# Adding the residual unscaled: a per-source deviation in the edge weights and in the second norm's epsilon

## The chip, the cores and the metric

The kernel runs on one core of a Trainium2 chip. The metric is the device time of one execution in microseconds (us). The kernel before takes 849.54 us, the median of three runs (848.42 to 850.84).

## What is computed

128 graphs of 128 nodes with 128 features go through two blocks. Each block has a residual and a layer norm without gain or bias:

```
x1 = layernorm(x + gnn0(x))      # two graph convolutions, then four LSTM passes over node windows
out = layernorm(x1 + gat(x1))    # multi-head attention over 256 edges
# gat: Xq = x1 Wlin', Xv = x1 Wval'                      (per node, 4 heads of 32)
#      e  = a . leaky_relu(Xq[src] + Xq[dst]) + log(adj[src, dst] + 1e-8)
#      w  = softmax of e over the edges of one source
#      Y[src] = sum over edges of w * Xv[dst];  gat = Y Wout'
# layernorm(z) = (z - mean(z)) / sqrt(var(z) + 1e-5)
```

The change concerns the second block only. Let y be the centred row x + gnn0(x) of one node, s = sqrt(var + eps) its deviation and r = 1/s. Then x1 = r y, and x1 + gat is the same row as y + s gat up to the factor r. A layer norm doesn't see that factor if its epsilon is multiplied by s squared.

## The kernel before

The core's five engines run hand-written instruction streams joined by semaphores. The first part (`front`) computes gnn0 and takes most of the time. The second part (`back`) is a software pipeline over 32 tiles of 4 graphs (`BT`), in 48 slots numbered n. Each engine has a function `slot(n)` that issues its share of several tiles at different depths, and the order within it is written out by hand.

In slot n of `back`:

- TensorE makes queries and values of tile n (L1330, L1352), edge scores of tile n-1 (L1373), the sum over end nodes of tile n (L1363, L1364), the sum by source of tile n-14 (`sum_by_source`, L1407), its output product (`output`, L1418), and turns tile n+1 or n+2 (L1326). Every eighth slot (13, 21, 29, 37) `attention_by_edge` turns the softmax row (L1387) and spreads r of the edges' end nodes over the edges (L1390).
- ScalarE (ACT in the profile) orders and copies tiles (L1522, L1526, L1533), scales queries (L1511, L1515), copies the sum by source (L1552), and normalises output tiles (L1547). For the late tiles 19 to 30 it also multiplies the kept row by r (`scale_x`, L1558).
- VectorE (DVE) takes the statistics of entering tiles (`stats_in`, L1620), scales queries, does the softmax steps (L1652 to L1676), weights gathered values (L1700), adds the residual (`add_mixed` of tile n-15: L1710 with r as a scalar in four instructions for tiles 0 to 18, L1707 in one instruction for the late tiles), and takes the statistics of leaving tiles (`stats_out`, L1718). `attention_out` (L1682, L1686) multiplies the attention by r of the end node.
- GpSimd (POOL) turns statistics into factors. `factors(n)` serves tile n+2 on its way in and tile n-15 on its way out in one set of small instructions: L1253, L1255, L1256, L1258, L1260, L1261, L1263, L1265, a power of -1/2 (L1267) and the shift (L1274). It also normalises half of each output tile up to tile 18 (L1240), and issues the additions and gathers by DMA.
- The DMA queue of SyncE stores values and output tiles.

A tile's query needs its factors from POOL, and TensorE's sum by source of a tile needs the residual add of the tile before (`o_read`). `stats_out` in slot n waits for `factors` of slot n-2. Entering tiles end with slot 31; slots 32 to 47 drain the rest. The last tile leaves by `leave_last` in two halves.

Of the kernel before, what the change touches and what calls it, by code (L numbers as in the profile page):

```python
# [103 lines left out]
def front(nc, sb, sem, tables, hT_hi, hT_lo, ident, adj_sb, psum, xb, adj, Wg0, bg0, Wg1, bg1, Wih, Whh, bih, bhh,  # L104
# [101 lines left out]
             "adjT_psum adjT_ready degree_psum degree_ready by_ready ranks_psum deg_hi bias_hi ranks_cut "  # L206
             "b_summed b_psum b_ready wg1_cut wg1_ready w_psum w_hi_ready w_lo_ready "
# [111 lines left out]
    def run_tensor(pe, entry):  # L319
# [96 lines left out]
        def slot(n):  # L416
# [33 lines left out]
            if has(n - 3):  # L450
                k = n - 3
                if not k:
                    pe.wait_ge(S["wg1_ready"], 1)
# [219 lines left out]
    def run_vector(dve, entry):  # L673
# [16 lines left out]
        def rank_rows():  # L690
            dve.wait_ge(S["ranks_psum"], 1)
            bank = psum[:, GATE_BANK[I], :]
            dve.tensor_copy(deg_rows[:, :, :], bank[0:RANKS, 0:P].unsqueeze(2).broadcast_to([RANKS, P, BT])).then_inc(S["deg_hi"], 1)
            dve.tensor_copy(bias_rows[:, :], bank[0:RANKS, P:2 * P]).then_inc(S["bias_hi"], 1)
            dve.wait_ge(S["deg_hi"], 1)
# [3 lines left out]
            dve.wait_ge(S["bias_hi"], 1)  # L699
            lo = slice(BIAS_LO, BIAS_LO + 2)  # L700
            dve.tensor_tensor(bias_rows[lo], bank[lo, P:2 * P], bias_rows[lo].bitcast(F32), ALU.subtract).then_inc(S["ranks_cut"], 1)
            dve.tensor_copy(wg1_hi[:, :], wg1[:, :]).then_inc(S["wg1_cut"], 1)
            dve.wait_ge(S["wg1_cut"], 1)
            dve.tensor_tensor(wg1_lo[:, :], wg1[:, :], wg1_hi[:, :].bitcast(F32), ALU.subtract).then_inc(S["wg1_ready"], 1)
# [311 lines left out]
def back(nc, sb, sem, tables, before, hT_hi, hT_lo, ident, psum, xt, a, src, v_rows, values, out):  # L1016
# [18 lines left out]
    RING = LAG + 13  # L1035
# [3 lines left out]
    LOG_AT, EXP_AT = 4, 6  # L1039
# [9 lines left out]
    x1_kept = sb("x1_kept", [P, RING, BT, P])  # L1049
    yT = sb("yT", [P, 2, TW])  # L1050
# [6 lines left out]
    diff, mean_sum, m2_sum, half_diff, minus_mean, m2_eps, diff_sq, var_eps = (  # L1057
        sb(n, [P, 2, BT]) for n in ("diff", "mean_sum", "m2_sum", "half_diff", "minus_mean", "m2_eps", "diff_sq", "var_eps"))

    rstd = sb("rstd", [P, tiles + LAG + 4, 2, BT])  # L1060
    shift = sb("shift", [P, 2, BT])
    edge_rstd = sb("edge_rstd", [P, EC, GT, BT])
# [10 lines left out]
             "edge_rstd_ready attn_ready va_ready yt_psum yT_ready scaled_x o_psum o_read stats2_done "  # L1073
# [73 lines left out]
    def scale_of(k, b):  # L1147
        return rstd[:, k, 0, b:b + 1]

    def out_factors(m, b):  # L1150
        return rstd[:, m + 4 + LAG, 1, b:b + 1], shift[:, m % 2, b:b + 1]
# [71 lines left out]
    def run_gpsimd(pool):  # L1223
# [19 lines left out]
        def factors(n):  # L1243
# [6 lines left out]
            if leaving:  # L1250
                pool.wait_ge(S["stats2_done"], n - 2 - LAG + 1)
            st = stats[:, n % 2, w]
# [12 lines left out]
            pool.tensor_tensor(var_eps[:, w], m2_eps[:, w], diff_sq[:, w], ALU.add).then_inc(S["var_done"], 1)  # L1265
            pool.wait_ge(S["var_done"], done)
            op = pool.tensor_tensor(rstd[:, n + 2, w], var_eps[:, w], minus_half[:, w], ALU.pow)  # L1267
            if leaving:
                op.then_inc(S["rstd_done"], 1)
                m = n - 2 - LAG  # L1270
# [3 lines left out]
                op = pool.tensor_tensor(shift[:, m % 2], minus_mean[:, 1], rstd[:, n + 2, 1], ALU.mult)  # L1274
            op.then_inc(S["factors_done"], 1)

# [43 lines left out]
    def tensor_steps(pe):  # L1320
# [61 lines left out]
        def attention_by_edge(g):  # L1382
            pe.wait_ge(S["attn_row"], g + 1)
            if g:
                pe.wait_ge(S["va_ready"], EC * g * GT)
            for c in range(EC):
                mm = pe.transpose(attn[:, c, :], row_a[:, c * P:(c + 1) * P], ident[:, :])  # L1387
            for c in range(EC):
                at = EC * P + c * GT * BT
                mm = pe.matmul(psum[:, ATTN, at:at + GT * BT], to_r[:, c * P:(c + 1) * P].bitcast(F32),  # L1390
                               rstd[:, g * GT:(g + 1) * GT, 0, :], start=True, stop=True)
            mm.then_inc(S["attn_psum"], 1)

# [45 lines left out]
        def slot(n):  # L1439
# [8 lines left out]
            if has(n):  # L1448
                values(n)
                if behind_values(n):  # L1450
                    last_query(n)
            if new_group and has(n):
# [52 lines left out]
    def scalar_steps(act):  # L1505
# [66 lines left out]
        def slot(n):  # L1572
# [18 lines left out]
            elif has(n - 1 - LAG):  # L1591
                copy_yT(n - 1 - LAG)
                if late(n - 1 - LAG):
                    scale_x(n - 1 - LAG)
# [19 lines left out]
    def vector_steps(dve):  # L1614
# [8 lines left out]
        def query_hi(k):  # L1623
            dve.wait_ge(S["factors_done"], k + 1)
            dve.wait_ge(S["q_psum"], 2 * k + 2)
            if k:
                dve.wait_ge(S["linear_kept"], k)
            dve.tensor_tensor(xq_hi[:, 0:IN_BANK, :], psum[:, Q, 0:IN_BANK * QC].rearrange("p (b d) -> p b d", d=QC),
                              rstd[:, k, 0, 0:IN_BANK].unsqueeze(2).broadcast_to([P, IN_BANK, QC]), ALU.mult)
# [47 lines left out]

        def attention_out(g):
# [3 lines left out]
            dve.tensor_copy(edge_rstd[:, :, :, :], bank[:, EC * P:EC * (P + GT * BT)].rearrange("p (c k b) -> p c k b", c=EC, b=BT)).then_inc(  # L1682
                S["edge_rstd_ready"], 1)
            dve.wait_ge(S["edge_rstd_ready"], g + 1)
            for c in range(EC):
                op = dve.tensor_tensor(attn[:, c, :].rearrange("p (b k h) -> p b k h", b=BT, h=HEADS),  # L1686
                                       bank[:, c * P:(c + 1) * P].rearrange("p (b k h) -> p b k h", b=BT, h=HEADS),
                                       edge_rstd[:, c].rearrange("p k b -> p b k").unsqueeze(3).broadcast_to([P, BT, GT, HEADS]), ALU.mult)
# [32 lines left out]
        def leave_last():  # L1721

            for h, of_half in enumerate(halves):
                dve.wait_ge(S["last_o"], h + 1)
                for b in of_half:
                    op = dve.scalar_tensor_tensor(out=x1_kept[:, place(last), b, :], in0=x1_kept[:, place(last), b, :],
                                                  scalar=scale_of(last, b), in1=psum[:, last_out_bank[h], b * P:(b + 1) * P],
                                                  op0=ALU.mult, op1=ALU.add)
                op.then_inc(S["last_added"], 1)
# [10 lines left out]
            dve.tensor_scalar(last_var[:, :], last_moments[:, :, 1], LN_EPS, None, ALU.add).then_inc(S["last_normed"], 1)  # L1740
# [19 lines left out]
        def slot(n):  # L1760
# [35 lines left out]
            for step in STEPS[part][1] if part is not None else ():  # L1796
                softmax(g, step)
            if n == 1:
# [101 lines left out]
```

## Time and profile before

| | |
|---|---|
| median of three runs | 849.54 us |
| the profiled execution, whole | 849.15 us |
| its span in the trace | 847.2 us |
| busy: PE, DVE, ACT, POOL | 818.1, 672.7, 616.4, 257.8 us |
| `back` takes over from `front` | about 601 us |
| slots 15 to 29 | about 670 to 772 us |
| last instruction of POOL ends | about 842.8 us |

A busy time is that of an engine's recorded instructions. In the rows, L numbers are lines of the kernel, "x4" joins four records, and the part in square brackets is idle time of the engine just before the instruction, with what ended it.

### The profile page before, as it was taken

The page shows a single profiled execution, that of the slowest core. Times are in us where ns is not written, and L with a number is a line of the kernel's source. Part 1 is how long each engine was busy: PE and PEld are TensorE (multiplying, and loading weights), DVE is VectorE, ACT ScalarE, POOL GpSimd, SP SyncE. Part 2 cuts the span into 40 slices and gives each one's busy share as a digit, 9 for nine tenths or more (in the row PEclk, how much of TensorE's full clock was granted, in tenths as well). Part 3 has the DMA queues.
Part 4 walks back from the last instruction along what each step waited for, and adds up shares of the span by engine and source line. Part 5 has one row for each costly group of instructions (what it writes and reads, how often), then busy time and mean ns, then how long its engine had stood idle before and what let it go on. Part 6 is the DMA issues. An engine that isn't in the chain of part 4 may idle for free.

```text
span 847.2 us, 14387 instructions
## 1 busy us (share of the span) xinstructions
PE 818.1 (97%) x4882; PEld 701.8 (83%) x4882; DVE 672.7 (79%) x1494; ACT 616.4 (73%) x1109; POOL 257.8 (30%) x604
## 2 busy tenths in 40 slices
PE   8999999999999999999999999999999999999883
PEld 7888888877888878988887888878887899999783
DVE  5888888868888788777787776768777799898884
ACT  3788778886677776777676566666697688887686
POOL 0233333350000000000000010100577577777886
PEclk9999999999999999999999999999999999999997
DMA  5122221000000000100000047777418866534543
GB/s 144 62 67 61 62 63 50 14 1 1 2 0 1 1 1 5 46 1 1 1 1 0 1 100 183 164 180 167 126 63 231 243 188 187 200 125 163 162 169 93
DMA packets 37895, 70.54 MB, mean 83 GB/s; under 512 B 3360, under 2 KB 24512, under 8 KB 32704
## 3 DMA queue, kind: packets, MB, share of 16 engines
q0 software_dynamic: 4608, 33.56, 15.3%
q1 hardware_dynamic: 32288, 35.73, 13.5%
q8 instruction: 40, 0.66, 0.3%
q10 hardware_dynamic: 928, 0.35, 0.2%
q14 instruction: 31, 0.25, 0.1%
HBM read 36.06 MB, written 16.78 MB: 62 GB/s over the span
## 4 chain that ended last, share of the span: by engine, by line
PE 82%; ACT 6%; POOL 6%; DVE 3%; issue 2%; DMA 1%; POOLq 0%; DVEq 0%; ACTq 0%
PE psum L514 9%; PE psum L515 9%; PE psum L516 9%; PE psum L532 7%; PE psum L528 7%; PE psum L529 6%; PE psum L1407 3%; PE psum L424 3%; PE psum L466 3%; PE psum L401 2%; PE psum L400 2%; PE psum L399 2%; PE psum L1330 2%; PE psum L1352 2%; PE psum L1363 2%
## 5 line engine op out<-in xcount | busy, mean ns | idle before, releaser
L654 ACT ACTIVATE work<-psum,bias 128x512 f32<-128x512 f32 (+2 forms) x364 | 229.0, 666 | 35.8 <-PE psum L532 31.8
L514 PE MATMUL psum<-hT_hi,w_hi 128*128 128x512 f32 (+2 forms) x362 | 139.6, 386 | 1.2 <-ACT work L654 1.2
L515 PE MATMUL psum<-hT_lo,w_hi 128*128 128x512 f32 (+2 forms) x362 | 139.3, 385 | 0.0
L516 PE MATMUL psum<-hT_hi,w_lo 128*128 128x512 f32 (+2 forms) x362 | 139.1, 384 | 0.0
L635 ACT ACTIVATE work<-work 128x512 f32<-128x512 f32 (+1 forms) x100 | 61.3, 613 | 94.9 <-DVE work L977 58.6
L1228 POOL DMA_DIRECT2D hT_lo<-hT_hi x8 | 7.6, 947 | 339.5 <-DVE hT_lo L924 320.2
L988 DVE TENSOR_TENSOR work<-work 128x512 f32<-128x512 f32 (+1 forms) x99 | 66.7, 673 | 47.7 <-ACT work L635 47.7
L528 PE MATMUL psum<-hs_hi,w_hi 128*128 128x512 f32 (+2 forms) x256 | 98.3, 384 | 0.3 <-DVE hs_hi L922 0.3
L532 PE MATMUL psum<-hs_lo,w_hi 128*128 128x512 f32 (+2 forms) x256 | 98.5, 385 | 0.0
L529 PE MATMUL psum<-hs_hi,w_lo 128*128 128x512 f32 (+2 forms) x256 | 97.8, 382 | 0.0
L970 DVE TENSOR_TENSOR work<-work 128x512 f32<-128x512 f32 (+1 forms) x100 | 66.4, 664 | 20.6 <-ACT work L654 20.5
L514 PEld LDWEIGHTS psum<-hT_hi,w_hi 128*128 128x128 f32 x362 | 68.3, 189 | 16.0 <-ACT work L654 1.5
L593 ACT ACTIVATE work<-psum,bias 128x512 f32<-128x512 f32 x96 | 65.7, 688 | 21.7 <-PE psum L401 19.0
L516 PEld LDWEIGHTS psum<-hT_hi,w_lo 128*128 128x128 f32 x362 | 68.2, 189 | 13.5
L515 PEld LDWEIGHTS psum<-hT_lo,w_hi 128*128 128x128 f32 x362 | 68.2, 188 | 13.0
L1407 PE MATMUL psum<-from_node,values 128*128 128x128 f32 x496 | 60.8, 276 | 5.1 <-DVE x_kept L1710 3.4
L1407 PEld LDWEIGHTS psum<-from_node,values 128*128 128x128 f32 x496 | 57.8, 192 | 5.8 <-issue 3.7
L1267 POOL TENSOR_TENSOR rstd<-var_eps,minus_half 128x4 f32<-128x4 f32 (+1 forms) x48 | 60.5, 1260 | 3.8
L314 POOL CAST hT_hi<-work 128x512 fp32r<-128x512 f32 x32 | 20.0, 624 | 125.3 <-DVE work L850 125.3
L532 PEld LDWEIGHTS psum<-hs_lo,w_hi 128*128 128x128 f32 x256 | 48.1, 188 | 11.2 <-DVE hs_lo L924 2.1
L528 PEld LDWEIGHTS psum<-hs_hi,w_hi 128*128 128x128 f32 x256 | 48.2, 188 | 10.3 <-DVE hs_hi L922 1.5
L529 PEld LDWEIGHTS psum<-hs_hi,w_lo 128*128 128x128 f32 x256 | 48.2, 188 | 9.2
(238 smaller groups left out, 1898.5 us busy)
## 6 DMA issues: line engine op xcount, KB each, us to landing
work<-x_by_batch SPq DMA_DIRECT2D x32, 256.0 KB, 2.6
x_stage<-x_by_state SPq DMA_DIRECT2D x8, 1024.0 KB, 5.7
hT_lo<-hT_hi POOLq DMA_DIRECT2D x8, 1024.0 KB, 8.7
hT_lo<-x_stage POOLq DMA_DIRECT2D x8, 1024.0 KB, 7.2
v_rows<-values SPq DMA_DIRECT2D x32, 256.0 KB, 2.4
out<-x_kept SPq DMA_DIRECT2D x31, 256.0 KB, 2.4
work<-L_gnn_Wih SPq DMA_DIRECT2D x4, 256.0 KB, 2.9
work<-L_gnn_Whh SPq DMA_DIRECT2D x3, 256.0 KB, 3.1
```

Source lines behind the costliest of these rows:

```text
L514: pe.matmul(out, w_hi[:, w, g, :], xh, start=True, stop=False)
L515: pe.matmul(out, w_hi[:, w, g, :], xl, start=False, stop=False)
L516: mm = pe.matmul(out, w_lo[:, w, g, :], xh, start=False, stop=(t == 0))
L528: pe.matmul(out, w_hi[:, w, g, :], hh, start=False, stop=False)
L529: pe.matmul(out, w_lo[:, w, g, :], hh, start=False, stop=False)
L532: pe.matmul(out, w_hi[:, w, g, :], hl, start=False, stop=True).then_inc(gate_psum[g], 1)
L593: op = act.activation(gate[1][g], psum[:, GATE_BANK[g], :], ACT.Tanh if g == G else ACT.Sigmoid, bias=bias[:, g:g + 1])
L635: act.activation(tanh_c[k % 2][:, 0:ph.width(tile)], cell[k % 2][:, 0:ph.width(tile)], ACT.Tanh).then_inc(S["tanh_ready"], 1)
L654: op = act.activation(gate[s][g][:, 0:ph.width(tile)], psum[:, 4 * s + g, 0:ph.width(tile)], ACT.Tanh if g == G else ACT.Sigmoid, bias=bia ...
L970: op = dve.tensor_tensor(i_g, gate[s][I][:, 0:ph.width(tile)], gate[s][G][:, 0:ph.width(tile)], ALU.mult)
L988: dve.tensor_tensor(h_full[s][:, 0:ph.width(tile)], gate[s][O][:, 0:ph.width(tile)], tanh_c[s][:, 0:ph.width(tile)], ALU.mult).then_inc(S[ ...
L1407: mm = pe.matmul(psum[:, sum_bank(k), b * P:(b + 1) * P], va_of(k, c, b), from_node[:, c, :], start=(c == 0), stop=(c == EC - 1))
```

## The change

The residual is added unscaled: `add_mixed` and `leave_last` add the attention's output to the kept row in one instruction per tile or half, and `scale_x` is gone. The edge weights are multiplied by s of the source as well as by r of the end node. For that, two transposes in slot 9 and one VectorE copy make the one-hot table of sources (`from_r`); GpSimd forms s and eps s^2 for eight tiles at a time (`late_scales`, slots 8, 16, 24, 32); TensorE spreads s over the edges by two more products a group; VectorE multiplies once more. GpSimd's `factors` adds the kept eps s^2 in an instruction of its own. The rings of factors and of kept rows are re-sized (26 to 25 kept rows), and a few semaphores of `front` are merged, with the same instructions between them.

```diff
 def factors(n):   # GpSimd, "leaving": a tile on its way out is served
             if leaving:
                 pool.tensor_scalar(minus_mean[:, 1], mean_sum[:, 1], -0.5, None, ALU.mult)
-            pool.tensor_scalar(m2_eps[:, w], m2_sum[:, w], 1.0 / P, LN_EPS, ALU.mult, ALU.add).then_inc(S["scaled"], 1)
+                pool.tensor_scalar(m2_mean[:, w], m2_sum[:, w], 1.0 / P, None, ALU.mult).then_inc(S["scaled"], 1)
+                pool.wait_ge(S["std_ready"], m // GT + 1)
+            else:
+                pool.tensor_scalar(m2_eps[:, w], m2_sum[:, w], 1.0 / P, LN_EPS, ALU.mult, ALU.add).then_inc(S["scaled"], 1)
             pool.wait_ge(S["scaled"], done)
+            if leaving:
+                pool.tensor_tensor(m2_eps[:, w], m2_mean[:, w], late_eps[:, m % KEPT, w], ALU.add)
             pool.tensor_tensor(diff_sq[:, w], half_diff[:, w], half_diff[:, w], ALU.mult).then_inc(S["squared"], 1)
...
+        def late_scales(g):
+            pool.wait_ge(S["factors_done"], GT * (g + 1))
+            if g:
+                pool.wait_ge(S["attn_psum"], g)
+            pool.tensor_tensor(std[:, :, :], var_kept[:, kept, 0], rstd[:, of_group, 0], ALU.mult)
+            pool.tensor_scalar(late_eps[:, kept, 1], var_kept[:, kept, 0], LN_EPS, None, ALU.mult).then_inc(S["std_ready"], 1)
...
 GpSimd, slot n, after factors(n)
+            if n and n % GT == 0 and n // GT <= groups:
+                if n == GT:
+                    pool.memset(late_eps[:, :, 0], LN_EPS)
+                late_scales(n // GT - 1)
...
         def attention_by_edge(g):
             pe.wait_ge(S["attn_row"], g + 1)
+            pe.wait_ge(S["std_ready"], g + 1)
...
+            for c in range(EC):
+                at = EC * P + (EC + c) * GT * BT
+                mm = pe.matmul(psum[:, ATTN, at:at + GT * BT], from_r[:, c * P:(c + 1) * P], std[:, :, :], start=True, stop=True)
             mm.then_inc(S["attn_psum"], 1)
+        def turn_sources():            # slot 9
+            for c in range(EC):
+                mm = pe.transpose(attn[:, c, :], from_node[:, c, :], ident[:, :])
+            mm.then_inc(S["from_psum"], 1)
...
-        def scale_x(m):
-            act.wait_ge(S["stats_done"], m + 1)
-            for b in range(BT):
-                kept = x1_kept[:, place(m), b, :]
-                op = act.activation(kept, kept, ACT.Copy, scale=scale_of(m, b))
-            op.then_inc(S["scaled_x"], 1)
...
+        def keep_sources():            # slot 9
+            dve.wait_ge(S["from_psum"], 1)
+            dve.tensor_copy(from_r[:, :], psum[:, ATTN, 0:E]).then_inc(S["from_ready"], 1)
...
 def attention_out(g):
+            dve.tensor_copy(edge_scale[:, :, :, :], of_ends[0]).then_inc(S["edge_scale_ready"], 1)
+            dve.wait_ge(S["edge_scale_ready"], 2 * g + 1)
+            dve.tensor_tensor(edge_scale[:, :, :, :], edge_scale[:, :, :, :], of_ends[1], ALU.mult).then_inc(S["edge_scale_ready"], 1)
...
         def add_mixed(m):
             dve.wait_ge(S["o_psum"], m + 1)
-            if late(m):
-                dve.wait_ge(S["scaled_x"], m - first_late + 1)
-                kept = x1_kept[:, place(m)]
-                dve.tensor_tensor(kept, kept, by_bank(out_bank(m)), ALU.add).then_inc(S["o_read"], 1)
-                return
-            for b in range(BT):
-                op = dve.scalar_tensor_tensor(out=x1_kept[:, place(m), b, :], in0=x1_kept[:, place(m), b, :], scalar=scale_of(m, b),
-                                              in1=psum[:, out_bank(m), b * P:(b + 1) * P], op0=ALU.mult, op1=ALU.add)
-            op.then_inc(S["o_read"], 1)
+            kept = x1_kept[:, place(m)]
+            dve.tensor_tensor(kept, kept, by_bank(out_bank(m)), ALU.add).then_inc(S["o_read"], 1)
```

## Rows read from the trace of the kernel before

**Rows 1.** The page: the chain that ended last, its shares by engine

```profile
PE 82%; ACT 6%; POOL 6%; DVE 3%; issue 2%; DMA 1%; POOLq 0%; DVEq 0%; ACTq 0%
```

**Rows 2.** Windows: stretch, length, busy us of PE, PEld, DVE, ACT, POOL; clock, DMA

```profile
666.00:774.00 108.00, 107.98 (x972) 99.48 (x973) 95.41 (x339) 88.70 (x186) 76.84 (x190) 1.00 0.56 182
...
812.00:843.00 31.00, 20.75 (x172) 19.44 (x171) 20.76 (x65) 27.11 (x76) 26.48 (x93) 0.91 0.31 98
```

**Rows 3.** Timeline of POOL: start us, length us, instruction; one round of `factors`

```profile
819.62 0.20 POOL L1253 TENSOR_TENSOR diff<-stats 128x4 f32<-128x4 f32 x1
819.77 0.20 POOL L1255 TENSOR_TENSOR mean_sum<-stats 128x4 f32<-128x4 f32 x1
...
820.22 0.23 POOL L1258 TENSOR_SCALAR half_diff<-diff 128x4 f32<-128x4 f32 x1
820.41 0.22 POOL L1260 TENSOR_SCALAR minus_mean<-mean_sum 128x4 f32<-128x4 f32 x1
820.69 0.19 POOL L1261 TENSOR_SCALAR m_eps<-m_sum 128x4 f32<-128x4 f32 x1
820.97 0.20 POOL L1263 TENSOR_TENSOR diff_sq<-half_diff 128x4 f32<-128x4 f32 x1
...
822.78 0.20 POOL L1253 TENSOR_TENSOR diff<-stats 128x4 f32<-128x4 f32 x1
```

**Rows 4.** Timeline around 772 us: what POOL's last idle time waited for

```profile
772.88 0.60 ACT L1533 ACTIVATE x_kept<-psum 128x512 f32<-128x512 f32 x1
...
773.51 0.87 DVE L1620 BATCH_NORM_STATS2 stats<-x_kept 128x6 f32<-128x128 f32 x4
...
774.46 0.21 POOL L1253 TENSOR_TENSOR diff<-stats 128x8 f32<-128x8 f32 x1 [2.42 <-DVE stats L1620]
```

**Rows 5.** Groups by line, all of `back`: count, busy us, mean ns

```profile
L1710 DVE SCALAR_TENSOR_TENSOR x_kept<-x_kept,rstd,psum 128x128 f32<-128x128 f32 x76 | 21.2, 341 | 8.4 <-PE psum L1418 8.3
...
L1240 POOL TENSOR_SCALAR x_kept<-x_kept,rstd,shift 128x128 f32<-128x128 f32 x38 | 18.7, 496 | 1.9 <-POOL shift L1274 0.2
...
L1558 ACT ACTIVATE x_kept<-x_kept,rstd 128x128 f32<-128x128 f32 x48 | 15.3, 398 | 0.0
...
L1707 DVE TENSOR_TENSOR x_kept<-x_kept,psum 128x512 f32<-128x512 f32 x12 | 8.1, 674 | 0.0
```

**Rows 6.** Timeline of PE, slot 29: attention by edge and what follows

```profile
767.16 0.38 PE L1387 MATMUL psum<-ident,row_a 128*128 128x128 f32 x2
767.38 0.53 PE L1390 MATMUL psum<-rstd,to_r 128*128 128x32 f32 x4
...
767.74 2.03 PE L1407 MATMUL psum<-from_node,values 128*128 128x128 f32 x16
```

**Rows 7.** Timeline of DVE, slots 9 and 13

```profile
646.04 0.57 DVE L1628 TENSOR_TENSOR xq_hi<-psum,rstd 128x396 fp32r<-128x396 f32 x1 [0.28 <-issue]
...
663.12 0.22 DVE L1682 COPY edge_rstd<-psum 128x64 f32<-128x64 f32 x1
663.38 0.50 DVE L1686 TENSOR_TENSOR psum<-psum,edge_rstd 128x128 f32<-128x128 f32 x2
```

**Rows 8.** Timeline of PE, slots 13 and 14

```profile
662.46 0.39 PE L1363 MATMUL psum<-ends,xq_hi 128*128 128x256 f32 x1 [0.50 <-DVE xq_lo L1643]
...
666.02 2.05 PE L1407 MATMUL psum<-from_node,values 128*128 128x128 f32 x16 [0.49 <-DVE values L1700]
```

**Rows 9.** Timeline of DVE and POOL around 791 us

```profile
791.23 0.69 DVE L1657 TENSOR_TENSOR_SCAN row_a<-cap_f,rows 128x256 f32<-128x256 f32 x1
...
791.36 0.57 POOL L1260 TENSOR_SCALAR minus_mean<-mean_sum 128x4 f32<-128x4 f32 x1
```

**Rows 10.** Timeline in the drain: PE, DVE, ACT

```profile
787.71 2.02 PE L1407 MATMUL psum<-from_node,values 128*128 128x128 f32 x16 [2.52 <-DVE x_kept L1710]
...
820.56 1.27 DVE L1700 TENSOR_TENSOR values<-values,psum 128x512 f32<-128x512 f32 x2
...
835.54 1.65 ACT L1547 ACTIVATE x_kept<-x_kept,shift,rstd 128x128 f32<-128x128 f32 x4 [0.85 <-POOL shift L1274]
```

More of the change, by code:

```diff
@@ L1034, in back @@
     LAG = GT + 5
-    RING = LAG + 13
+    RING = LAG + 12
+    FACTORS, KEPT = 3 * GT, 2 * GT
     GROUP = before.phases[-1].sizes[0] // BT
@@ L1049, in back @@
     x1_kept = sb("x1_kept", [P, RING, BT, P])
+    from_r = sb("from_r", [P, E])
+    late_eps = sb("late_eps", [P, KEPT, 2, BT])
+    std = sb("std", [P, GT, BT])
+    spare = sb("spare", [P, 96])
     yT = sb("yT", [P, 2, TW])
@@ L1056, in back @@
     stats = sb("stats", [P, 2, 2, BT, 6])
-    diff, mean_sum, m2_sum, half_diff, minus_mean, m2_eps, diff_sq, var_eps = (
-        sb(n, [P, 2, BT]) for n in ("diff", "mean_sum", "m2_sum", "half_diff", "minus_mean", "m2_eps", "diff_sq", "var_eps"))
-    rstd = sb("rstd", [P, tiles + LAG + 4, 2, BT])
+    diff, mean_sum, m2_sum, half_diff, minus_mean, m2_mean, m2_eps, diff_sq = (
+        sb(n, [P, 2, BT]) for n in ("diff", "mean_sum", "m2_sum", "half_diff", "minus_mean", "m2_mean", "m2_eps", "diff_sq"))
+    rstd = sb("rstd", [P, FACTORS, 2, BT])
+    var_kept = sb("var_kept", [P, KEPT, 2, BT])
     shift = sb("shift", [P, 2, BT])
-    edge_rstd = sb("edge_rstd", [P, EC, GT, BT])
+    edge_scale = sb("edge_scale", [P, EC, GT, BT])
     last_stats, last_moments = sb("last_stats", [P, BT, 6]), sb("last_moments", [P, BT, 2])
@@ L1072, in back @@
              "z_psum leaky_ready edges_psum log_taken log_added max_f max_b below_max exp_done sum_f sum_b recip_done attn_row attn_psum "
-             "edge_rstd_ready attn_ready va_ready yt_psum yT_ready scaled_x o_psum o_read stats2_done "
+             "edge_scale_ready attn_ready va_ready yt_psum yT_ready from_psum from_ready std_ready o_psum o_read stats2_done "
              "halves scaled squared var_done rstd_done factors_done out_act out_pool "
@@ L1147, in scale_of @@
     def scale_of(k, b):
-        return rstd[:, k, 0, b:b + 1]
+        return rstd[:, k % FACTORS, 0, b:b + 1]
     def out_factors(m, b):
-        return rstd[:, m + 4 + LAG, 1, b:b + 1], shift[:, m % 2, b:b + 1]
+        return rstd[:, (m + 4 + LAG) % FACTORS, 1, b:b + 1], shift[:, m % 2, b:b + 1]
     def region_free(engine):
@@ L1251, in factors @@
                 pool.wait_ge(S["stats2_done"], n - 2 - LAG + 1)
+            m = n - 2 - LAG
+            at, kept = (n + 2) % FACTORS, (n + 2) % KEPT
             st = stats[:, n % 2, w]
@@ L1260, in factors @@
                 pool.tensor_scalar(minus_mean[:, 1], mean_sum[:, 1], -0.5, None, ALU.mult)
-            pool.tensor_scalar(m2_eps[:, w], m2_sum[:, w], 1.0 / P, LN_EPS, ALU.mult, ALU.add).then_inc(S["scaled"], 1)
+                pool.tensor_scalar(m2_mean[:, w], m2_sum[:, w], 1.0 / P, None, ALU.mult).then_inc(S["scaled"], 1)
+                pool.wait_ge(S["std_ready"], m // GT + 1)
+            else:
+                pool.tensor_scalar(m2_eps[:, w], m2_sum[:, w], 1.0 / P, LN_EPS, ALU.mult, ALU.add).then_inc(S["scaled"], 1)
             pool.wait_ge(S["scaled"], done)
+            if leaving:
+                pool.tensor_tensor(m2_eps[:, w], m2_mean[:, w], late_eps[:, m % KEPT, w], ALU.add)
             pool.tensor_tensor(diff_sq[:, w], half_diff[:, w], half_diff[:, w], ALU.mult).then_inc(S["squared"], 1)
             pool.wait_ge(S["squared"], done)
-            pool.tensor_tensor(var_eps[:, w], m2_eps[:, w], diff_sq[:, w], ALU.add).then_inc(S["var_done"], 1)
+            pool.tensor_tensor(var_kept[:, kept, w], m2_eps[:, w], diff_sq[:, w], ALU.add).then_inc(S["var_done"], 1)
             pool.wait_ge(S["var_done"], done)
-            op = pool.tensor_tensor(rstd[:, n + 2, w], var_eps[:, w], minus_half[:, w], ALU.pow)
+            op = pool.tensor_tensor(rstd[:, at, w], var_kept[:, kept, w], minus_half[:, w], ALU.pow)
             if leaving:
                 op.then_inc(S["rstd_done"], 1)
-                m = n - 2 - LAG
                 pool.wait_ge(S["rstd_done"], m + 1)
@@ L1273, in factors @@
                     pool.wait_ge(S["out_act"], m - 1)
-                op = pool.tensor_tensor(shift[:, m % 2], minus_mean[:, 1], rstd[:, n + 2, 1], ALU.mult)
+                op = pool.tensor_tensor(shift[:, m % 2], minus_mean[:, 1], rstd[:, at, 1], ALU.mult)
             op.then_inc(S["factors_done"], 1)
+        def late_scales(g):
+            of_group, kept = slice(g * GT % FACTORS, g * GT % FACTORS + GT), slice(g * GT % KEPT, g * GT % KEPT + GT)
+            pool.wait_ge(S["factors_done"], GT * (g + 1))
[3 more added lines that the diff above has]
+            pool.tensor_scalar(late_eps[:, kept, 1], var_kept[:, kept, 0], LN_EPS, None, ALU.mult).then_inc(S["std_ready"], 1)
         def gather_values(j):
@@ L1451, in slot @@
                     last_query(n)
+            if n == SOURCES_AT:
+                turn_sources()
             if new_group and has(n):
@@ L1681, in attention_out @@
             dve.wait_ge(S["attn_psum"], g + 1)
-            dve.tensor_copy(edge_rstd[:, :, :, :], bank[:, EC * P:EC * (P + GT * BT)].rearrange("p (c k b) -> p c k b", c=EC, b=BT)).then_inc(
-                S["edge_rstd_ready"], 1)
-            dve.wait_ge(S["edge_rstd_ready"], g + 1)
+            of_ends = [bank[:, EC * P + j * EC * GT * BT:EC * P + (j + 1) * EC * GT * BT].rearrange("p (c k b) -> p c k b", c=EC, b=BT)
+                       for j in range(2)]
+            dve.tensor_copy(edge_scale[:, :, :, :], of_ends[0]).then_inc(S["edge_scale_ready"], 1)
+            dve.wait_ge(S["edge_scale_ready"], 2 * g + 1)
+            dve.tensor_tensor(edge_scale[:, :, :, :], edge_scale[:, :, :, :], of_ends[1], ALU.mult).then_inc(S["edge_scale_ready"], 1)
+            dve.wait_ge(S["edge_scale_ready"], 2 * g + 2)
             for c in range(EC):
@@ L1724, in leave_last @@
                 dve.wait_ge(S["last_o"], h + 1)
[L1725 to L1729, printed above, removed]
+                at = slice(of_half.start, of_half.stop)
+                kept = x1_kept[:, place(last), at, :]
+                dve.tensor_tensor(kept, kept, by_bank(last_out_bank[h])[:, at, :], ALU.add).then_inc(S["last_added"], 1)
             for h, of_half in enumerate(halves):
@@ L1739, in leave_last @@
             dve.wait_ge(S["last_normed"], 2)
-            dve.tensor_scalar(last_var[:, :], last_moments[:, :, 1], LN_EPS, None, ALU.add).then_inc(S["last_normed"], 1)
+            dve.wait_ge(S["std_ready"], groups)
+            dve.tensor_tensor(last_var[:, :], last_moments[:, :, 1], late_eps[:, last % KEPT, 1], ALU.add).then_inc(S["last_normed"], 1)
             dve.wait_ge(S["last_scaled"], 1)
@@ L1797, in slot @@
                 softmax(g, step)
+            if n == SOURCES_AT:
+                keep_sources()
             if n == 1:
```

32 lines of the change are left out of this document (16 added, 16 removed).

## The prediction

> **What bounds the kernel now.** I began with the page's shares and its chain of waits. PE has 82% of the chain, ACT and POOL 6% each, DVE 3% [rows 1]. The two engines that the change relieves, ACT and DVE, are the question; so I cut `back` into stretches (the view by windows) and read the timeline of each engine in them. The median is 849.54 us; the profiled execution took 849.15, so sums made on it are carried over to the median by adding the difference that they give. The kernel can be told from an unchanged one from about 0.3%, 2.55 us, on.
>
> Stretch A, slots 15 to 29, 666 to 774 us: PE is busy 107.98 of 108.00 us at full clock, DVE 95.41, POOL 76.84 [rows 2]. Whatever leaves DVE there is worth nothing unless PE waits for it, and what is added to PE counts in full.
>
> Stretch B, from 774.46 us to the end of POOL's work at about 842.8 us: POOL waits for the last time at 774.46 us, for the statistics of slot 30 [rows 4]. From there its timeline has no idle time but the short issue gaps around two pairs of gathers. It makes 17 rounds of `factors` (n = 29 to 45), up to n = 34 with the normalising of half a tile between them. In the drain a round takes 822.78 - 819.62 = 3.16 us [rows 3], again and again. ACT's round is as long by chance: a copy step of 0.5, four scalings (4 x 0.398 = 1.6 as lengths, about 1.17 in steps), four normalisings of 1.65. But at 835.54 it is ACT that waits, 0.85 us, for POOL's shift [rows 10], and POOL, which waits for nobody, is the last to finish. So the view of the chain, which names ACT for part of the drain, has two equally long loops to choose from, and only POOL's reaches back to 774 us unbroken.
>
> **The change part by part.**
>
> *Removed from ACT:* 48 scalings, 12 tiles of 4 [rows 5]. All lie in stretch B, next to a POOL that is never free. Worth 0; if POOL were not there, see the second rival.
>
> *Removed from DVE:* 76 scaled additions (19 tiles of four, 0.341 us each; in the timeline a tile steps on by about 1.12 us) become 19 whole ones as L1707, 0.674 us [rows 5]. That is 0.45 us a tile, 8.5 us of DVE time. In stretch A PE is full, so 0. At the seam, slot 30: the statistics of tile 31 start at 773.51, after the addition, but also only after ACT's copy of the tile, which ends at 772.88 + 0.60 = 773.48 [rows 4]. An earlier addition leaves the start where it is: 0. In stretch B PE does wait for an addition, 2.52 us before 787.71 [rows 10], but PE is not what ends the stretch: 0 again. The last tile's two halves gain some tenths beside POOL's last rounds: 0.
>
> *Added to PE:* each group gets two more products of the form L1390 (two matmuls, four records). The old ones take from 767.38 to 767.74, 0.36 us [rows 6]; the two transposes of slot 9 are priced by L1387, 767.38 - 767.16 = 0.22 us [rows 6]. Place by place:
> - slot 9: 0.22. PE runs without a gap there. The copy that DVE adds in that slot (about 0.4 us) falls on 0.28 us of idle time [rows 7] plus the 0.22 us by which PE is itself later, so it is covered.
> - slot 13: PE waits 0.50 us for xq_lo behind the attention [rows 8], which hides the 0.36. But DVE's additional multiplication sits between the copy and the weighting: one step of 663.38 - 663.12 = 0.26 us [rows 7], and at 666.02 PE waits 0.49 us for exactly those weighted values [rows 8]. So 0.26.
> - slots 21 and 29: 0.36 each, PE being full. DVE's step of 0.26 there is less than the 0.45 it saves in the same slot.
> - slot 37: in stretch B, beside POOL: 0.
> Sum on PE: 0.22 + 0.26 + 0.36 + 0.36 = 1.20 us. Bounds: 0.7 (only slots 21 and 29 count) to 1.5.
>
> *Added to POOL, in each leaving round:* before, minus_mean to m_eps takes 0.28 us and m_eps to diff_sq 0.28 [rows 3], the second across a wait. After, m2_mean takes the place of m_eps but has one operation, as minus_mean has after half_diff, where the step is 0.19 [rows 3]. Its length should be like minus_mean's, 0.03 more than m_eps, so the step across the wait becomes 0.31. Then m2_eps, a two-input instruction with no wait before diff_sq: a step as from diff to mean_sum, 0.15 to 0.16 [rows 3]. New: 0.19 + 0.31 + 0.155 = 0.65 against 0.56, so +0.09 a round. The added wait for `std_ready` was satisfied slots ago (late_scales of that group ran at least 7 slots before), and everything queued behind it waits for m2_mean anyhow. Bounds for a round: 0.06 (m2_mean as short as m_eps) and 0.25 (two operations or one make no difference, and the additional wait costs 0.1). I take 0.09, since each of its steps has a like step in the same round. 17 rounds: 1.5 us, from 1.0 to 4.3. In stretch A the rounds have slack (POOL 71% busy [rows 2]): 0.
>
> *Added to POOL, late_scales:* groups 0 to 2 fall into slots 8, 16 and 24, where POOL has waits to spare: 0. The fourth falls into slot 32, inside stretch B, after the round and before a normalising: two instructions of 128x32. They lie between 0.20 us (128x4 [rows 3]) and 0.50 (128x128, L1240 [rows 5]) each; nearer the first, 0.22, so about 0.45 us for the pair, bounds 0.3 to 1.0. Its wait for attn_psum is long met (slot 29). Behind it in POOL's queue stand normalise_out and the next round, so all of it counts.
>
> *What the phase does:* at 791.36 minus_mean took 0.57 instead of 0.22, ending just as DVE's scan of 791.23 + 0.69 does [rows 9]. Five POOL instructions between 791 and 801 us are stretched like this, 1.8 us together, each beside a DVE instruction of the fourth softmax with both inputs in SBUF. Those DVE instructions stay, but DVE will be about 0.5 to 1 us earlier against POOL's rounds. If all of them fell on POOL's long power, 1.8 us would be won; if none did, about 1 us more be lost. I book 0. The Trainium skill (SBUF — State Buffer, section "SBUF: two separate sides") says the same of the mechanism: VectorE with two SBUF inputs and GpSimd take one port pair in turn, and the loser waits for the whole instruction. By that rule the new additions, which read one operand from PSUM, block POOL no more than the old ones; no row here contradicts it, since the stretched ones stand beside scans and SBUF-only products alone.
>
> [...]
>
> Sum: 1.20 + 1.5 + 0.45 = 3.15 us. 849.15 + 3.15 = 852.3 for the profiled execution; on the median 849.54 + 3.1 = 852.6, or 0.36% slower.
>
> **The rivals.**
>
> *Most of it is hidden (no change that can be measured).* PE's additions count in slots 21 and 29 only (0.7), the rounds cost 1.0, late_scales 0.3, and DVE's earlier scans fall on POOL's power for 0.9 us: 0.7 + 1.0 + 0.3 - 0.9 = +1.1, 850.7. For it: PE has stalls in slots 13 and 14 [rows 8]. Against: POOL's additions lie on an engine that never idles.
>
> *ACT sets the drain (faster).* If the chain's reading is right and POOL merely keeps step with ACT, then 12 rounds of 3.16 us lose ACT's scaling, and the next loop is DVE's: two weightings 1.27 [rows 10], an addition 0.67, four statistics 0.87 as in [rows 4], 2.8 us. 12 x 0.37 = 4.4 us won, 1.2 lost on PE: -3.3, 846.3. It decides from the point on where POOL's round could be shorter than ACT's. Against it: POOL's steps are the same 3.16 with ACT waiting for it as without, and the 0.85 us of ACT [rows 10].
>
> *POOL pays more.* The upper bounds of the round: 17 x 0.25 = 4.3, with 1.2 and 0.6: +6.1, 855.7. For it: a wait more per round, and two where the order of satisfied and open waits is new. Against: the added wait has been satisfied for several slots when POOL reaches it, and it comes while m2_mean is still running.
>
> **How the numbers follow.** The forecast 0.55 (its own range 851.3 to 854.5; 0.45 of it beyond 2.55 us, 0.10 within); hidden 0.29; ACT's drain 0.07, of which 0.01 within; POOL pays more 0.09. Slower 0.45 + 0.09 = 0.54; same 0.10 + 0.29 + 0.01 = 0.40; faster 0.06. Eight in ten: 849.9 to 855.3, from below the hidden case to just short of the dearest one.
>
> **What would show it.** The slots of stretch A at the same PE step (about 6.7 us) with L1390's sibling 0.36 us longer in slots 21 and 29, POOL's last idle time about 1.2 us later than 774.46; POOL's round 3.25 in the drain with ACT now waiting for the shift in every round; no L1558, and DVE and PE idle more. I am wrong if POOL shows idle time in its rounds after slot 30 or its round is shorter than 3.16; if POOL's last idle time comes no later; or if the first instruction that waits for the added `std_ready` does so for a measurable time.

## The result and the profile after

The changed kernel takes 853.32 us, the median of 13 runs (851.99 to 853.80), against 849.54 us before (13 runs, 848.22 to 851.13). The ratio is 1.0043, with a 95% interval of 1.0035 to 1.0051: 3.7 us slower. Forecast were 852.6 us and slower.

Seen coarsely, the pages differ by what the change says: ACT is busy 603.8 us (616.4 before) and DVE 666.5 (672.7), PE 824.4 (818.1) and POOL 262.5 (257.8), in a span of 851.6 (847.2). The chain of waits of the changed kernel, shares by engine, no longer gives ACT its 6% [rows 1]:

```profile
PE 82%; POOL 8%; ACT 3%; DVE 3%; issue 2%; DMA 0%; POOLq 0%; DVEq 0%; ACTq 0%
```

One round of `factors` in the drain, timeline of POOL of the changed kernel (start, length, instruction), against [rows 3]:

```profile
829.56 0.20 POOL L1261 TENSOR_TENSOR diff<-stats 128x4 f32<-128x4 f32 x1
...
830.35 0.22 POOL L1268 TENSOR_SCALAR minus_mean<-mean_sum 128x4 f32<-128x4 f32 x1
830.53 0.22 POOL L1269 TENSOR_SCALAR m_mean<-m_sum 128x4 f32<-128x4 f32 x1
830.90 0.20 POOL L1275 TENSOR_TENSOR m_eps<-m_mean,late_eps 128x4 f32<-128x4 f32 x1
831.05 0.20 POOL L1276 TENSOR_TENSOR diff_sq<-half_diff 128x4 f32<-128x4 f32 x1
...
832.87 0.20 POOL L1261 TENSOR_TENSOR diff<-stats 128x4 f32<-128x4 f32 x1
```

The round takes 832.87 - 829.56 = 3.31 us where it took 3.16. m_mean starts 0.18 after minus_mean (0.28 for m_eps before), m_eps 0.37 after m_mean, diff_sq 0.15 after m_eps.

`late_scales` in slot 32 and POOL's last idle time, same view, with one line of the timeline of DVE at the end:

```profile
776.33 0.21 POOL L1261 TENSOR_TENSOR diff<-stats 128x8 f32<-128x8 f32 x1 [2.71 <-DVE stats L1649]
...
796.23 0.20 POOL L1286 TENSOR_TENSOR shift<-minus_mean,rstd 128x4 f32<-128x4 f32 x1
796.38 0.25 POOL L1295 TENSOR_TENSOR std<-var_kept,rstd 128x32 f32<-128x32 f32 x1
796.70 0.31 POOL L1296 TENSOR_SCALAR late_eps<-var_kept 128x32 f32<-128x32 f32 x1
796.98 1.24 POOL L1246 TENSOR_SCALAR x_kept<-x_kept,rstd,shift 128x128 f32<-128x128 f32 x2
797.21 0.76 DVE L1689 TENSOR_TENSOR_SCAN row_b<-cap_b,row_a 128x256 f32<-128x256 f32 x1
```

Normalising now starts 0.75 us after the shift. In the kernel before that step is 0.31 us in the same slot (793.95 to 794.26), so the pair costs 0.44. The last two lines show the stretching of [rows 9] too: the two rows of a half tile take 1.24 us there and 0.88 elsewhere, and a scan of DVE with two SBUF inputs stands beside them from 797.21 to 797.97.

PE in slot 21 of the changed kernel, against [rows 6] (the two differ only in slot):

```profile
714.18 0.53 PE L1418 MATMUL psum<-rstd,to_r 128*128 128x32 f32 x4
714.54 0.61 PE L1422 MATMUL psum<-std,from_r 128*128 128x32 f32 x4
714.99 2.03 PE L1443 MATMUL psum<-from_node,values 128*128 128x128 f32 x16
```

From the first record of one line to the first of the next, the old products take 0.36 and the new ones 0.45. That is a matter of the place and not of the table. The same view from 714.38 us and from 715.36 us on leaves out the first record of the old products and that of the sum by source:

```profile
714.21 0.50 PE L1418 MATMUL psum<-rstd,to_r 128*128 128x32 f32 x3
...
715.18 1.84 PE L1443 MATMUL psum<-from_node,values 128*128 128x128 f32 x15
```

The second old record starts 0.03 us after the first (714.18, 714.21), every later one of both tables 0.11 us after the one before it, and the second record of the sum 0.19 us after its first (714.99, 715.18). So each of the eight narrow records costs 0.11 us, 0.45 for four; of the old four, 0.08 us stands in the line behind them. In the kernel before it is the same (the first two records of [rows 6]'s L1390 start at 767.38 and 767.41, those of its L1407 at 767.74 and 767.94).

How this adds up can be read from the start of the values product of each slot (L1352 before, L1377 after); the difference between the two executions moves only at four places:

| slots | later than before, us | what lies at the step |
|---|---|---|
| 0 to 9 | 0.48 | the front part, see e8_front_only |
| 10 to 14 | 0.69 to 0.73 | transposes in slot 9: 0.21 |
| 15 to 21 | 0.97 | DVE's added product ahead of slot 14's wait: 0.25 |
| 22 to 29 | 1.42 | added products in slot 21: 0.45 |
| 30, 31 | 1.86 | added products in slot 29: 0.44 |

And ACT, relieved of its scalings, waits. The view of the waits from 776 us on (engine and line, waited for: us in total, times, longest), first of the kernel before:

```profile
ACT x_kept L1547 <- POOL shift L1274: 7.3, 5, 2.8
...
ACT x_kept L1585 <- POOL shift L1286: 16.6, 11, 4.4
```

One thing in this profile is not explained by the change's code. TensorE's granted clock was at the lower of its two levels (1.2 and not 2.4 GHz) from 790.5 to 793.9 us, which it was not in the profile of the kernel before. The view by windows, PE alone (stretch, length, busy us, granted clock, DMA), the kernel before first:

```profile
790.50:793.90 3.40, 2.91 (x26) 1.00 0.75 257
...
790.50:793.90 3.40, 3.40 (x21) 0.50 0.87 321
```

Ahead of it PE had waited 2.10 us for DVE's addition, up to 789.16; in the kernel before it waited 2.52 us at that place [rows 10] and the clock stayed up. The profiles of e4_no_pool_part (789.1 to 792.5) and e5_after_act_norm (787.6 to 791.0) have such a fall, those of the other kernels have none between 785 and 800 us, the changed kernel's relatives e2, e3, e7 and e10 among them. So no run shows that the change brings it. Here it makes DVE wait 3.55 us for PE's scores ahead of the softmax at 793.47, where it waited 2.30 before; POOL waits for none of them there and isn't held up, but DVE's scans come later against its rounds.

**Bookkeeping.** Two numbers of each profiled execution carry the reading: A, the start of POOL's round after its last long wait (774.46 before), and B, from there to the start of its last power (`last_rstd`, 841.79 before). A contains the front part, which differs between executions of any kernel; B doesn't. Of the time, the ratio with its interval is the safer reading: the executions of one kernel fall into groups (of the kernel before, near 848.2, 849.4 and 850.9 us), so that a median of a few can jump by 1 us.

| kernel | time, us | ratio to before (95%) | A | B | round |
|---|---|---|---|---|---|
| before | 849.54 | | 774.46 | 67.33 | 3.16 |
| changed | 853.32 | 1.0043 (1.0035 to 1.0051) | 776.33 | 69.78 | 3.31 |
| e1_no_scaling | 848.46 | 0.9993 (0.9984 to 1.0001) | 773.55 | 67.02 | 3.16 |
| e2_no_source_scale | 852.16 | 1.0031 (1.0020 to 1.0043) | 775.07 | 69.88 | 3.31 |
| e3_wait_ahead | 852.13 | 1.0033 (1.0021 to 1.0046) | 776.62 | 69.05 | 3.24 |
| e4_no_pool_part | 849.92 | 1.0012 (1.0004 to 1.0021) | 775.06 | 67.41 | 3.16 |
| e8_front_only | 849.38 | 1.0004 (0.9995 to 1.0013) | 774.52 | 67.33 | 3.17 |
| e5_after_act_norm | 851.31 | 1.0027 (1.0014 to 1.0039) | 774.75 | 69.04 | 3.31 |
| e6_before_act_norm | 848.47 | 0.9996 (0.9986 to 1.0006) | 774.68 | 66.39 | 3.16 |
| e7_both | 850.27 | 1.0013 (1.0003 to 1.0022) | 776.00 | 66.56 | 3.24 |
| e11_before_order_alone | 848.02 | 0.9986 (0.9977 to 0.9995) | 773.43 | 67.05 | 3.16 |
| e9_before_order | 847.21 | 0.9965 (0.9952 to 0.9979) | 774.71 | 65.21 | 3.17 |
| e10_after_order | 848.76 | 0.9985 (0.9976 to 0.9994) | 776.46 | 65.53 | 3.26 |
| e12_no_scaling_order | 846.51 | 0.9965 (0.9953 to 0.9977) | 775.11 | 64.29 | 3.17 |

Each was timed in five rounds against the kernel before, whose own medians were 849.05 to 849.54. B of the changed kernel is 2.45 us longer: 17 rounds x 0.15 = 2.55, late_scales 0.44, and 0.5 back by how DVE's two-input instructions fall on POOL's (between 790 and 803 us five of POOL's are stretched in either kernel, by 1.8 us together before and by 1.2 in the changed one). A less the start of slot 0 leaves the front part out: it is 169.2 to 169.3 us in all eight kernels without PE's part and 170.6 to 170.7 in all six with it.

### The profile page after: what moved, and what is told of

It is laid out like the page before. It is cut to its first block, busy times and chain, and to the rows that moved or that the text cites. A ratio compares the mean times of both kernels' runs of the same rounds, so it can differ in the third digit from the quotient of the medians.

```text
span 851.6 us, 14386 instructions
## 1 busy us (share of the span) xinstructions
PE 824.4 (97%) x4900; PEld 707.5 (83%) x4900; DVE 666.5 (78%) x1440; ACT 603.8 (71%) x1061; POOL 262.5 (31%) x644
## 4 chain that ended last, share of the span: by engine, by line
PE 82%; POOL 8%; ACT 3%; DVE 3%; issue 2%; DMA 0%; POOLq 0%; DVEq 0%; ACTq 0%
PE psum L514 9%; PE psum L515 9%; PE psum L516 9%; PE psum L532 7%; PE psum L528 7%; PE psum L529 6%; PE psum L424 4%; PE psum L1443 3%; PE psum L466 3%; PE psum L401 2%; PE psum L399 2%; PE psum L400 2%; PE psum L1355 2%; POOL rstd L1280 2%; PE psum L1377 2%
## 5 line engine op out<-in xcount | busy, mean ns | idle before, releaser
L515 PEld LDWEIGHTS psum<-hT_lo,w_hi 128*128 128x128 f32 x362 | 68.1, 188 | 13.1
L1443 PE MATMUL psum<-from_node,values 128*128 128x128 f32 x496 | 63.8, 284 | 4.4 <-DVE values L1736 2.2
L1443 PEld LDWEIGHTS psum<-from_node,values 128*128 128x128 f32 x496 | 60.7, 200 | 5.2 <-DVE values L1736 4.9
L1280 POOL TENSOR_TENSOR rstd<-var_kept,minus_half 128x4 f32<-128x4 f32 (+1 forms) x48 | 59.5, 1240 | 3.8
```

The lines of the kernel that those rows point to most:

```text
L515: pe.matmul(out, w_hi[:, w, g, :], xl, start=False, stop=False)
L1280: op = pool.tensor_tensor(rstd[:, at, w], var_kept[:, kept, w], minus_half[:, w], ALU.pow)
L1443: mm = pe.matmul(psum[:, sum_bank(k), b * P:(b + 1) * P], va_of(k, c, b), from_node[:, c, :], start=(c == 0), stop=(c == EC - 1))
```

## The experiments

**Is the relief of ACT and DVE worth anything?** The kernel before, without any scaling of the kept rows:

```diff
         def add_mixed(m):
-            if late(m):
-                dve.wait_ge(S["scaled_x"], m - first_late + 1)
...
+            kept = x1_kept[:, place(m)]
+            dve.tensor_tensor(kept, kept, by_bank(out_bank(m)), ALU.add).then_inc(S["o_read"], 1)
...
-                if late(n - 1 - LAG):
-                    scale_x(n - 1 - LAG)
```

> The kernel before, with the scaling of the kept rows left out (no scaling on ACT for tiles 19 to 30, a plain whole-tile addition on VectorE for tiles 0 to 30), so what is added to the attention's output is the unscaled row; nothing else changes. If POOL's unbroken run from slot 29 on sets the end, the relief of ACT and DVE is worth nothing: 849.5, within 0.7 us of before. If ACT sets the drain, as the chain of waits named it, it is 3 to 5 us faster: about 846.

Measured 848.46 us, ratio 0.9993, interval 0.9984 to 1.0001: at most 1.4 us, and no difference can be told. B is 67.02 against 67.33, the round the same 3.16 us. 13.1 us of busy ACT time (616.4 to 603.3) and 7.7 us of DVE time (672.7 to 665.0) left the kernel for no gain that can be told. The rival in which ACT sets the drain is out.

**What does PE's part cost?** The changed kernel without the deviation of the source in the edge weights:

```diff
-                mm = pe.matmul(psum[:, ATTN, at:at + GT * BT], from_r[:, c * P:(c + 1) * P], std[:, :, :], start=True, stop=True)
...
-                turn_sources()
...
-                keep_sources()
...
-            dve.tensor_tensor(edge_scale[:, :, :, :], edge_scale[:, :, :, :], of_ends[1], ALU.mult).then_inc(S["edge_scale_ready"], 1)
```

> The changed kernel, with the deviation of the source left out of the edge weights: no transposes and copy in slot 9, no two added products a group on PE, no added multiplication on DVE; GpSimd's additions stay. By the traces PE's place by place delays sum to 0.21 (slot 9) + 0.25 (slot 14) + 0.45 (slot 21) + 0.44 (slot 29) = 1.35 us, all ahead of stretch B: 1.35 us less than the changed kernel's 853.3, so 852.0. If PE's additions were hidden, 853.3.

Measured 852.16 us, 1.16 below the changed kernel (1.0 by the ratios, whose intervals overlap: the trace has to decide). The slots' starts are now later than before by the same amount from slot 0 (0.58) to slot 31 (0.61): all four steps of the table are gone. B is 69.88, like the changed kernel's, so PE's part acts on A alone.

**Does the satisfied wait cost something?**

```diff
 def factors(n):
             entering, leaving = has(n + 2), 0 <= n - 2 - LAG < last
+            if leaving and (n - 2 - LAG) % GT == 0:
+                pool.wait_ge(S["std_ready"], (n - 2 - LAG) // GT + 1)
...
-                pool.wait_ge(S["std_ready"], m // GT + 1)
```

> The changed kernel, with GpSimd's wait for std_ready made once a group ahead of the round and not in each round between m2_mean and m2_eps. The step across the wait is 0.37 us in the changed kernel where I expected 0.31. If the second wait costs the 0.06 to 0.07, the round falls from 3.31 to 3.24 us and 17 rounds save 1.1 us: 852.2. If an already satisfied wait costs nothing (the theory of the prediction) the time stays at 853.3 and the 0.37 is due to m2_mean.

Measured 852.13 us, 1.2 below the changed kernel; by the ratios it is 0.9, and their intervals overlap, so the time alone doesn't show a gain. The timeline of POOL in this kernel:

```profile
827.16 0.22 POOL L1271 TENSOR_SCALAR m_mean<-m_sum 128x4 f32<-128x4 f32 x1
827.46 0.20 POOL L1276 TENSOR_TENSOR m_eps<-m_mean,late_eps 128x4 f32<-128x4 f32 x1
```

The step from m_mean to m_eps falls from 0.37 to 0.30, and the round to 3.24. So this wait, whose count was reached slots ago, costs 0.07 us where it stands between an instruction and one that depends on it. 17 x 0.07 = 1.2 us would be gained by it; B falls by only 0.73, the scans again falling otherwise (the shift of slot 32 takes 0.51 us here, at 796.41, and 0.20 in the changed kernel).

**What does POOL's part cost?** The changed kernel with `factors` as before and constants for s and the second epsilon:

```diff
-                pool.tensor_scalar(m2_mean[:, w], m2_sum[:, w], 1.0 / P, None, ALU.mult).then_inc(S["scaled"], 1)
-                pool.wait_ge(S["std_ready"], m // GT + 1)
-            else:
-                pool.tensor_scalar(m2_eps[:, w], ...
+            pool.tensor_scalar(m2_eps[:, w], m2_sum[:, w], 1.0 / P, LN_EPS, ALU.mult, ALU.add).then_inc(S["scaled"], 1)
...
-                late_scales(n // GT - 1)
+                pool.memset(std[:, :, :], 1.0)
+                pool.memset(late_eps[:, :, :], LN_EPS).then_inc(S["std_ready"], 1)
```

> The changed kernel, with GpSimd's part left out: factors as before, no late_scales; s is a constant 1 and the second norm's epsilon unscaled. PE's and DVE's additions stay. If POOL's additions are 17 x 0.15 + 0.6 = 3.1 us and nothing hides them: 853.3 - 3.1 = 850.2, or up to 0.6 us more since the stretched instructions of slots 32 to 34 fall otherwise. If the cost is all on PE or in front: 853.

Measured 849.92 us, 3.4 below the changed kernel, B back at 67.41. Against the kernel before the ratio is 1.0012 (0.4 to 1.8 us), PE's part. The two parts together, 1.2 + 3.4 = 4.6, are somewhat more than the 3.7 to be explained; the uncertainty of each is near 1 us, and by the ratios they are 1.0 + 2.6 = 3.6. POOL is not quite unbroken here: at 796.16 it waits 0.39 us for DVE's statistics, after the lower clock of 789.1 to 792.5 us.

**Is the 0.48 us ahead of slot 0 the merged semaphores?** The kernel before, with the front part of the changed one:

```diff
-            dve.wait_ge(S["deg_hi"], 1)
+            dve.wait_ge(S["ranks_hi"], 1)
...
-                    pe.wait_ge(S["wg1_ready"], 1)
+                    pe.wait_ge(S["wg1_ready"], 2)
```

> The kernel before with only the merged semaphores of the front part from the changed one. In the profiled executions the back part begins 0.49 us later in the changed kernel. If that is the merged semaphores, 850.0; if it is how executions of any kernel differ from one another (others lie at -0.9 to +0.8 us there), 849.5 as before.

Measured 849.38 us, 1.0004 (0.9995 to 1.0013): no cost that can be told, at most 1.1 us. In its profile slot 0 starts 0.08 us later than before, and in those of all the others between 1.1 us earlier (e5_after_act_norm) and 0.8 us later (e3_wait_ahead).

**Where is time to be had?** If POOL sets stretch B, work that ACT can do should leave it. Two kernels, from the changed one and from the one before:

```diff
+    def by_act_alone(m):
+        return m >= 15
...
-            if has(n - 3 - LAG) and not late(n - 3 - LAG):
+            if has(n - 3 - LAG) and not by_act_alone(n - 3 - LAG):
                 normalize_out(n, n - 3 - LAG)
...
-            for b in range(BT if late(m) else HALF):
+            for b in range(BT if by_act_alone(m) else HALF):
```

> The changed kernel, with output tiles 15 to 18 normalised wholly by ACT and not half by GpSimd: four pairs of L1240 leave POOL's run in slots 31 to 34, each a step of about 1.0 us (0.85 and a wait). If POOL alone sets the end there, 853.3 - 4.0 = 849.3. VectorE has 3.55 us of idle time in one piece and little else between 784 and 812 us, and comes next: if it takes over, the gain is 2.5 to 3.5, so 850 to 851.

Measured 851.31 us: 2.0 less (1.4 by the ratios), short of both numbers. Of the 4 us that left POOL, 2.95 came back as waits: 1.08 for ACT's normalising (793.53) and 1.87 for DVE's statistics (796.18). The profile has the lower clock from 787.6 to 791.0 us, in which PE's sum by source takes 3.65 us and not 2.02, so a part of the second wait may belong to this execution alone (e7_both below, without the fall at that place, waits 1.08 us there).

> The kernel before with the same move (output tiles 15 to 18 normalised wholly by ACT). POOL theory alone: 849.5 - 4.0 = 845.5. Here VectorE is busy 33 of 38 us between 774 and 812 us with the scaled additions still on it and ACT's round is as long as POOL's: if these take over, the gain is 2 to 2.5: about 847.3. If ACT's round sets the end it isn't faster at all.

Measured 848.47 us, 0.9996: nothing that can be told, where 2 to 4 us were expected. The timeline of POOL of e6_before_act_norm shows where it went:

```profile
792.25 0.20 POOL L1277 TENSOR_TENSOR shift<-minus_mean,rstd 128x4 f32<-128x4 f32 x1 [0.44 <-ACT x_kept L1550]
...
795.33 0.51 POOL L1256 TENSOR_TENSOR diff<-stats 128x4 f32<-128x4 f32 x1 [2.88 <-DVE stats L1721]
```

Of the 4 us that left POOL, 3.3 came back as waits, 2.88 of it for DVE's statistics of slot 33. In slot 32 DVE weights two tiles ahead (four instructions, 2.5 us) before the addition for which PE waits (the 2.52 us of [rows 10]); whether that makes the statistics late is tried below.

With the wait ahead of the round as well, from the changed kernel:

> The changed kernel with both: the wait for std_ready once a group, ahead of the round, and output tiles 15 to 18 normalised wholly by ACT. If the two add up: 852.1 - (gain of the second alone, 2.5 to 4) = 848.1 to 849.6. The relief of ACT and DVE could be worth something only here, where POOL is shorter.

Measured 850.27 us, 3.05 below the changed kernel; the second measure gave 1.9 on top of e3. The added up range of 848.1 to 849.6 was missed for a like reason: POOL waits 1.08 us for DVE in slot 33.

**Is it DVE's order?** In slot 32 the weightings of tiles 19 and 20 go behind the addition and the statistics:

```diff
-            if not new_group:
+            if not new_group and n != tiles:
                 for k in ahead:
                     weight_values(k, 0)
                     weight_values(k, 1)
...
                 stats_out(n, n - 2 - LAG)
+            if n == tiles:
+                for k in ahead:
+                    weight_values(k, 0)
+                    weight_values(k, 1)
```

> The kernel before with output tiles 15 to 18 normalised by ACT alone, and in slot 32 VectorE weights tiles 19 and 20 after its residual addition and statistics and not ahead of them. Moving the normalising alone gave 0.6 us, since POOL then waited 2.9 us for VectorE's statistics behind the four weightings (2.5 us). If that wait is what ate the gain, this is 2 to 3 us faster than that kernel: 846. If POOL's run isn't what sets the end once shortened (ACT's equally long round), 848.5.

Measured 847.21 us, ratio 0.9965 (0.9952 to 0.9979): the fastest of the kernels that leave nothing out, 2.3 us below the kernel before (3.0 by the ratio), though not the 846 that I expected. The order accounts for a part of the wait: it fell from 2.88 to 1.81 us, and B by 1.18. The addition of slot 32 no longer stands behind the four weightings, but at 785.48 it waits 1.09 us for PE's output product.

> The changed kernel with the wait ahead of the round, tiles 15 to 18 normalised by ACT alone, and the same order on VectorE in slot 32. It had 850.3 us without the order, with POOL waiting 1.1 us for VectorE there: 1 us or a little more less, 849. Compared with the previous one, POOL's 17 x 0.08 + 0.6 and PE's 1.35 us remain as the change's cost, 3.3 us in all, unless ACT's free time is now worth something.

Measured 848.76 us, 0.9985. Faster than the kernel before, but 1.6 us behind its sister, and not 3.3. A says where: 776.46 against 774.71, PE's part of about 1.4 us and the front. B is 65.53 against 65.21: nearly equal, though a round is 0.09 longer. POOL's waits for DVE in the two, both from the timeline of POOL; first e9_before_order:

```profile
794.19 0.51 POOL L1256 TENSOR_TENSOR diff<-stats 128x4 f32<-128x4 f32 x1 [1.81 <-DVE stats L1721]
```

In e10_after_order the same instruction starts at 795.63 with no idle time before it, behind a stretched `late_scales`:

```profile
794.88 0.79 POOL L1300 TENSOR_SCALAR late_eps<-var_kept 128x32 f32<-128x32 f32 x1
795.63 0.45 POOL L1266 TENSOR_TENSOR diff<-stats 128x4 f32<-128x4 f32 x1
```

> The kernel before with VectorE's order in slot 32 alone. POOL is never idle there, so by the theory an earlier VectorE is worth nothing but for how its scans fall on POOL's instructions: 849.3, within 1 us either way. By the rival (PE's 2.52 us wait for the addition is on the path) 847.

Measured 848.02 us, 0.9986 (0.9977 to 0.9995). This lies between the two expectations and is a small gain that B doesn't explain: 67.05 against 67.33. The rest of the span's difference lies ahead of A in that execution, nearly all of it (0.99 us) ahead of slot 0. It remains open whether the order alone is worth more than some tenths.

**Does the relief pay once POOL is shorter?**

> The kernel before with output tiles 15 to 18 normalised by ACT alone and VectorE's order in slot 32, and with the scaling of the kept rows left out as in e1_no_scaling. With POOL unbroken the relief was worth nothing. In e9_before_order POOL waits 1.81 us once for VectorE's statistics, behind the scaled additions and the weightings; in the changed kernel's sister (e10_after_order) that wait is gone. If the relief pays where POOL is shortened, POOL's run from its last wait of slot 30 to its last power falls from 65.21 to about 63.5 us and the time to 845.7. If the wait has another cause, 847.2 stays.

In its timeline POOL's wait of slot 33 is 0.82 us:

```profile
793.68 0.51 POOL L1256 TENSOR_TENSOR diff<-stats 128x4 f32<-128x4 f32 x1 [0.82 <-DVE stats L1712]
```

The wait fell by 1.0 us and B by 0.92, to 64.29, half of what I expected. The median is 846.51 against 847.21 of e9, the ratios to before are the same 0.9965: in the profile the relief has become worth about 1 us, in the time it can't be told from none.

## Why the prediction was right, step by step

- *PE full in stretch A, its additions counted in full.* Right. The places were the four named; slot 9's 0.22 was 0.21, slot 14's 0.26 was 0.25. Slots 21 and 29 cost 0.45 and 0.44 and not 0.36, and the sum is 1.35 and not 1.20. The reading of [rows 6] was at fault and not the likeness: the step of 0.36 from L1390 to L1407 holds one record start of 0.03 us, and the 0.08 that it lacks stand in L1407's first step of 0.19.
- *POOL unbroken from slot 30's wait to the end; ACT and DVE relieved for nothing.* Right: e1_no_scaling shows it for the relief, and e4_no_pool_part shows the other side, as 2.6 to 3.4 us go with POOL's additions. One run is left over: e11_before_order_alone, 0.4 to 2.0 us faster though nothing was taken off POOL and B is only 0.28 shorter.
- *POOL's round +0.09.* The mis-sized term: it was +0.15, 17 x 0.06 = 1.0 us too little. The step with the one-operation m2_mean (0.18 to 0.19) and the step to diff_sq (0.15) were as read; the step across the wait was 0.37 and not 0.31. The sentence that failed is that the added wait costs nothing because it was satisfied slots ago. e3_wait_ahead removes 0.07 with it and then shows the round that was forecast, 3.24. One of the prediction's own signs of being wrong, a measurable time at the added wait, did come. The rival "POOL pays more" had the right mechanism, with a price of 0.1 for the wait and the rest of its bound unneeded. The 0.15 is made up of +0.15 for the added instruction, -0.09 for the operation saved, and +0.09 across the wait.
- *late_scales 0.45.* Measured 0.44.
- *The phase of DVE's scans 0.* It gave back about 0.5 us. The Trainium skill (SBUF — State Buffer, "SBUF: two separate sides") says that a VectorE instruction with two SBUF inputs and a GpSimd instruction that reads SBUF share a pair of ports, and that the one that starts first has the pair for its whole instruction and blocks the other. The trace agrees: the small stretched instructions end with DVE's, as minus_mean at 791.36 + 0.57 = 791.93 with the scan at 791.23 + 0.69 = 791.92 [rows 9]. How many are hit couldn't be read ahead, and in the changed kernel's profile it also hung on the lower clock ahead of the scans.
- *The sum.* 1.35 + 2.55 + 0.44 - 0.5 = 3.8 us for 3.7 measured; forecast was 3.15. The forecast was 1.0 too low for the rounds and 0.15 too low for PE, and 0.5 too high for the phase. That the last made up for half of the others is luck.

## What to carry to other kernels

A busy share of 30% of the whole can hide an engine that is never idle for the last 70 us: in the kernel before, POOL is busy 58.1 of the 69 us from 774 to 843 us, more than any other engine there (DVE 54.0, PE 52.9, ACT 52.1). Look for the last idle time of each engine and ask which of them runs unbroken from there to the end: only what is taken off that one counts, and what is added to it counts at once, 0.15 us in a round of ten small instructions being 2.5 us here. When two loops have equal length the chain of waits may name the wrong one, as it named ACT's here; the one that can be relieved without gain (e1_no_scaling) is not the bound. And after work was moved off that engine, waits for the others took back 3.3 of 4 us. DVE's order of slot 32 was 1.1 of that (e9_before_order) and the scaled additions 1.0 (e12_no_scaling_order); what the last 0.8 us of POOL's wait hang on wasn't tried.

## What was unexpected of the hardware

A satisfied semaphore wait on POOL between m2_mean and the instruction that depends on it costs 0.07 us a time (0.37 against 0.30 in e3_wait_ahead). And the step on PE from one line's first record to the next one's can be 0.08 us short where narrow products (128x32) follow wide ones (0.36 for four records of 0.11), with the 0.08 in the line behind.
